# Four linear layers on one core: two products of layer 0 and the up projection change places in TensorE's order

## The reference, cut to what matters

```
x = x + (x @ W0[subject].T + b0[subject])            # layer 0, 512 x 512
x = x + rotate_pairs_of_rows(x, amplitudes ** dt, frequencies * dt)   # layer 1
x = x + (x @ W2[category] + b2[category])            # layer 2, 512 x 512
h = relu(x @ W1[language] + b1[language])            # layer 3, 512 -> 128
y = x + (h @ Wup[language] + bup[language])          #          128 -> 512
x = x + layernorm(y) * gamma[language] + beta[language]
```

## Time and profile before

| | |
|---|---|
| median of 3 runs | 1144.45 us (1143.76 to 1145.31) |
| the profiled execution | 1143.54 us, of which the span from first to last instruction is 1141.1 us |
| TensorE matmuls busy | 1102.6 us, 97% of the span |
| VectorE busy | 916.4 us, 80% |
| ScalarE busy | 778.7 us, 68% |
| GpSimd busy | 677.9 us, 59% |
| mean granted clock of TensorE | 0.992 |
| DMA | 353.5 MB, 310 GB/s on average |

### The profile page before, as it was taken

How to read it: one execution, slowest core, us unless ns; L and a number is a source line. 1 busy time by engine, 2 the same in 40 slices (tenths; PEclk the granted TensorE clock), 3 DMA queues, 4 the chain that set the end, 5 groups by cost and what they waited for, 6 DMA issues and landing times.

```text
span 1141.1 us, 28378 instructions
## 1 busy us (share of the span) xinstructions
PE 1102.6 (97%) x6046; PEld 924.0 (81%) x6046; DVE 916.4 (80%) x1373; ACT 778.7 (68%) x1824; POOL 677.9 (59%) x807
## 2 busy tenths in 40 slices
PE   4799999999999999999999999999999999999996
PEld 2588888888788888888888888887888888787885
DVE  7787787778987787778978877878877878888876
ACT  3476776767676776767767666767767767676764
POOL 5756556557755656556656556566556566565563
PEclk9899999999999999999999999999999999999999
DMA  7898979897998999799989889988998999798882
GB/s 247 307 330 302 321 284 334 315 309 277 381 338 295 322 316 315 269 351 327 333 303 361 307 275 341 323 300 308 356 310 286 342 316 356 263 369 323 312 297 70
DMA packets 97554, 353.50 MB, mean 310 GB/s; under 512 B 11870, under 2 KB 12510, under 8 KB 79932
## 3 DMA queue, kind: packets, MB, share of 16 engines
q1 hardware_dynamic: 95756, 350.39, 86.7%
q10 hardware_dynamic: 1584, 0.93, 0.3%
HBM read 316.94 MB, written 34.34 MB: 308 GB/s over the span
## 4 chain that ended last, share of the span: by engine, by line
PE 92%; DVE 2%; issue 2%; ACT 1%; DMA 1%; POOL 1%; DVEq 0%; SPq 0%; POOLq 0%; ACTq 0%
PE ps_mix L1075 10%; PE ps_l L1064 10%; PE ps_l L1100 10%; PE ps_l L1048 10%; PE ps_l L1094 10%; PE ps_l L1090 10%; PE ps_hT L1120 9%; PE ps_l L1059 5%; PE ps_x3T L1110 5%; PE ps_l L1052 5%; PE ps_y L1133 3%; PE ps_y L1131 3%; PE ps_y L1130 3%; DVE w_lo L873 1%; DMA x_in<-xT 1%
## 5 line engine op out<-in xcount | busy, mean ns | idle before, releaser
L595 ACT ACTIVATE w_hi<-w_in 128x1024 fp32r<-128x1024 f32 x256 | 270.8, 1058 | 219.5 <-POOL w_in L469 219.5
L873 DVE TENSOR_TENSOR w_lo<-w_in,w_hi 128x1024 fp32r<-128x1024 f32 x256 | 333.7, 1303 | 19.8 <-ACT w_hi L595 18.1
L482 POOL TENSOR_SCALAR var_eps<-square_sum 128x1 f32<-128x1 f32 x128 | 24.4, 191 | 414.5 <-DVE w_lo L873 307.9
L902 DVE TENSOR_TENSOR x<-ps_l,rows 128x512 f32<-128x512 f32 x126 | 87.0, 691 | 124.3 <-PE ps_l L1100 124.3
L640 ACT ACTIVATE x3T<-ps_x3T,minus_bup 128x128 f32<-128x128 f32 x512 | 145.8, 366 | 49.3 <-PE ps_x3T L1110 48.0
L508 POOL TENSOR_TENSOR x_beta<-x,rows 128x512 f32<-128x512 f32 x128 | 168.8, 1319 | 0.0
L476 POOL TENSOR_TENSOR x_lo<-x_in,x_hi 128x512 fp32r<-128x512 f32 x127 | 164.1, 1292 | 7.5 <-ACT x_hi L571 7.5
L469 POOL TENSOR_TENSOR w_in<-w_in,ident 128x512 f32<-128x512 f32 x128 | 166.5, 1301 | 2.9 <-DMA w_in<-W 2.9
L1075 PEld LDWEIGHTS ps_mix<-mix,x 128*128 128x128 f32 x1024 | 125.0, 192 | 32.9 <-issue 32.8
L1048 PE MATMUL ps_l<-w_hi,x_hi 128*128 128x512 f32 x512 | 150.2, 415 | 0.0
L1075 PE MATMUL ps_mix<-mix,x 128*128 128x128 f32 x1024 | 141.9, 282 | 4.9 <-DVE x L883 4.9
(11 more groups left out here) (148 smaller groups left out, 1843.7 us busy)
## 6 DMA issues: line engine op xcount, KB each, us to landing
w_in<-W SPq DMA_DIRECT2D x128, 1024.0 KB, 6.6
rows<-sample_rows SPq DMA_DIRECT2D x128, 768.0 KB, 7.1
x_in<-xT SPq DMA_DIRECT2D x128, 256.0 KB, 6.2
w_in<-W SPq DMA_DIRECT2D x128, 256.0 KB, 5.0
out<-yb SPq DMA_DIRECT2D x128, 256.0 KB, 6.6
w_in<-W0T SPq DMA_DIRECT2D x7, 1024.0 KB, 5.5
wup_sb<-Wup SPq DMA_DIRECT2D x1, 2560.0 KB, 13.7
w_in<-W0T SPq DMA_DIRECT2D x4, 512.0 KB, 6.4
```

The costliest lines, as they stand in the source:

```text
L595: act.activation(w2_hi[:, halves[n]], w2_in[s % WB][:, halves[n]], ACT.Copy).then_inc(w2_hi_made, 1)
L873: dve.tensor_tensor(w2_lo[:, half], w2_in[s % WB][:, half], w2_hi[:, half].bitcast(fp32), ALU.subtract).then_inc(w2_lo_made, 1)
```

## The change

`l0_back` loses its first two matmuls, which become `l0_middle`. `l2` is cut in two behind L1094: `l2_front` and `l2_back`. In the loop TensorE now takes `l0_middle(s + 1)` between the two. The load of the language offset moves with it, ahead of `l0_middle`. From s = 2 on the up projection comes ahead of the transposes; at s = 1 their order stays. What each stage computes and waits for is the same, and so are the instructions of all other engines.

```diff
-            def l0_back(s):
-
+            def l0_middle(s):
 
                 for c in range(C // 2, C):
                     pe.matmul(ps_l0[:, :], x_lo[s % 2][:, c * N:(c + 1) * N], w0_hi[s % 2][:, c * D:(c + 1) * D],
                               start=False, stop=False)
+
+            def l0_back(s):
+
+
                 for c in range(C):
...
-            def l2(s):
+            def l2_front(s):
...
                 mm.then_inc(l2_hi_done, 1)
+
+            def l2_back(s):
+
                 for c in range(C):
...
             for s in range(1, B):
                 if s < LAST:
                     l0_front(s + 1)
-                l2(s)
+                l2_front(s)
+                here = language_offset(pe, s - 1)
+                if s < LAST:
+                    l0_middle(s + 1)
+                l2_back(s)
                 if s == 1:
                     sort_coefficients()
-                here = language_offset(pe, s - 1)
                 if s < LAST:
                     l0_back(s + 1)
-                transpose_x3(s)
                 if s == 1:
+                    transpose_x3(s)
                     pe.wait_ge(wup_hi_made, len(wup_parts))
                     pe.wait_ge(wup_lo_made, len(wup_parts))
                     pe.wait_ge(coef_made, 2)
                 up(s - 1, here)
+                if s > 1:
+                    transpose_x3(s)
                 if s < LAST:
                     rotate(s + 1)
                 down(s)
```

More of the change, by code:

```diff
@@ L1135, in _ @@
             l0_front(0)
+            l0_middle(0)
             l0_back(0)
@@ L1139, in _ @@
             gather_rows()
-            l2(0)
+            l2_front(0)
+            l2_back(0)
             gather_beta()
@@ L1143, in _ @@
             l0_front(1)
+            l0_middle(1)
             l0_back(1)
```

## The result

| | before | after |
|---|---|---|
| median | 1144.88 us (4 runs) | 1179.37 us (4 runs, 1179.09 to 1180.61) |
| ratio | | 1.0303, 95% interval 1.029 to 1.0315 |
| profiled execution, its span | 1143.54, 1141.1 us | 1179.35, 1177.4 us |
| median time from rotation to rotation | 8.43 us | 8.73 us |

What follows compares the result with a forecast made beforehand. TensorE's fixed matmul chain bounds the kernel, with no cover for x1 at the rotation. 117 x 0.30 = 35.1 plus 0.8 us for slow steps gives 35.9; on 1143.54 that is 1179.4, stated as 1180, range 1172 to 1200.

Steps and rivals of the forecast that it cites:

- What bounds it: Steady step: a fixed chain of TensorE matmuls, 8.44 us between rotations, with no cover left for x1 at the rotation.
- A slack of about 0.16 us: DVE's chain L902, L935, L883 to x1 could come about 0.16 us later before the change.
- x1 did cost: Rotation's weight load before the change: its wait for x1 was said to cost almost nothing, with gaps in 123 steps.
- L883 overlaps L935 by 0.08: DVE's queue after the change: L883 starts 0.08 before L935 ends, as L935 does with L902.
- E: The end of layer 2 in a step, from which the prediction counts its times in us.
- the rival of 1189 us: DVE's queue: L883 doesn't overlap L935, so the step grows by 0.37 or 0.38 us; 1189 us, chance 0.14.
- Rotation at E + 2.18, a step of 0.29: Rotation's first matmul waits for x1 until E + 2.18 against 1.89 us of work; step grows 0.29, taken as 0.30.
- The slow steps: The 8 steps not steady: h_lo's wait makes them lose 0.1 rather than gain 0.36, together 0.8 us.
- The transposes cost nothing as long as x1 holds the rotation back: Transposes just ahead of the rotation: copies of x3T keep 0.2 us of slack before the down projection's fourth chunk.
- The floor beneath: Down projection: if x1 were early, the x3T copies bind, 0.1 a step, 12 us, 1156 us; rival's chance 0.04.
- What would show it: New profile: TensorE idle before rotation released by x1, 0.3 us a step, 30 to 40 us together; 8.74 between rotations.
- The clock: TensorE: its clock falls because it idles in every step; 80 us, 1260 us, chance 0.02.

Runs made afterwards that it cites:

- x1 first: VectorE makes x1 (finish_l0) ahead of finish_norm: 1146.34 us in the kernel before the change, 1157.53 us in the kernel after it.
- the late wait written first: The kernel before, with the wait for l0_done written first in finish_l0: 1140.9 us, ratio 0.9968.
- the last experiment: The kernel after, with GpSimd making h_lo ahead of the fold of the next W2: 1178.19 us, ratio 1.0296.
- part 1 alone: The kernel after, with the transposes back ahead of the up projection, so only the two x_lo products are moved: 1178.29 us, ratio 1.0298.
- part 2 alone: The kernel before, with only the up projection put ahead of the transposes: 1153.41 us, ratio 1.0086.
- part 1 with x1 first: The kernel before, with the two x_lo products moved and VectorE making x1 ahead of finish_norm; transposes stay ahead of up: 1157.97 us, ratio 1.012.

## Why the prediction was right, point by point

- **What bounds it.** A fixed chain of matmuls with no cover left at the rotation: right. Counted from rotation to rotation, 116 steps grew by 0.30 each, 34.9 of the span's 36.3 us.
- **"A slack of about 0.16 us".** Right as far as tested: one small operation used up 0.08 of it without any cost to the step, and a move of one product, 0.23, cost 0.07. x1 first gained the steady step nothing in the kernel before. "Costs almost nothing" was a little low: x1 did cost 0.03 a step, as the late wait written first showed.
- **L883 overlaps L935 by 0.08.** Forecast E + 1.31 for its start and E + 2.00 for its end; measured E + 1.31 and E + 1.99. This refutes the rival of 1189 us. The Trainium skill, "VectorE: DVE Perf Modes", section "The DRAIN you can't avoid", has the next operation start when the pipe is empty; the rows of this step have two pairs that start 0.08 ahead of the listed end. Its section "Two Vector instructions with no wait between them" allows such a start to an instruction that isn't held, and with that the trace agrees. By the first rule alone, at the price that the rival gives, the kernel would have taken 1189 us.
- **Rotation at E + 2.18, a step of 0.29.** Two errors that cancelled. The load came 0.11 behind x1 and the matmul 0.03 behind the load, not 0.12 and 0.06: E + 2.13, which is 0.24 by itself. The other 0.06 lie behind the rotation: from it to the end of the next layer 2 it took 6.10 us before and 610.87 - 604.26 - 0.45 = 6.16 after. Half of that is in the rotation: with its first load later, its first matmul to that of down is 0.97 (604.26 to 605.23 in that timeline) instead of 0.94. Most of the rest is in the x2T_hi products, 0.93 instead of 0.91 from their first to the first x2T_lo product; why is open. I hadn't priced either.
- **The slow steps.** "0.1 each, 0.8 us together": wrong, and the sum came out by luck. The seven steps with a new W0 changed by -0.5 to +0.2 us and are 0.4 us shorter together. What the span has beyond the steady steps is the one step at the start, 2.0 us longer at the lower granted clock, where the prediction had "changes of a tenth". The mechanism (w_lo's wait shrinks, h_lo's appears) is in the rows; as the last experiment shows, it is worth about 1 us.
- **"The transposes cost nothing as long as x1 holds the rotation back".** Right in this kernel (part 1 alone and both parts differ by 1 us). The floor beneath is real, too: part 2 alone stands on it, and so does x1 first. Its price was somewhat high, 0.1 a step and 12 us for 0.07 and 8 us: the copies' signal is there 0.06 behind their end, not 0.1. That x1 first came out near the 1156 us of that rival (1157.5) is partly luck, since some 5 us of it lie in the slow steps and at the start.
- **"What would show it".** Wrong in one place: I had said that TensorE's idle time would be listed as released by x1. The waits list it as a gap of the *weight load*, "issue", 34.1 us against 26.9, only 7 us more; 2.2 of 230 us show up as idle of PE. The sure signs were the time from rotation to rotation, and the number of matmuls in a stretch. DVE's wait before L902 grew to 1.61, its steady wait for the up projection is gone, and w_lo's waits fell from 5.7 to 1.7 us, all as said.
- **The clock** stayed at 1.00 in the even stretch though TensorE loses 0.3 us in each step. What it did cost is the 2 us at the start, behind an idle time of 4.5 us that both kernels have. The Trainium skill, "TensorE: Matmul & The Clock Gate", section "A second HAM failure mode: psum-queue depth-cycling", describes a kernel in which short idles between groups let the clock swing; the ones here didn't.

What failed clearly were two expectations behind the prediction, for part 2 alone and for part 1 with x1 first. Both took away the wait that bound and assumed nothing close behind it. With one part or the other in place, three chains are late by little: x1 by 0.24 us (part 1), x3 into the transposes by 0.13 (part 1 without part 2), the copies of x3T by 0.06 (part 2).

## What to carry to other kernels

When two products change places on the engine that bounds the kernel, its own work stays the same and its consumers' deadlines don't: count, from the end of each product that someone waits for, how much work is left before the result comes back, and compare it with the whole queue of the consumer (here 1.89 us against 2.13). Do it for every chain that closes within a few tenths, since a fix for one only uncovers the next. And look at how many instructions a stretch holds, not at how busy it reads: part 1 alone is 230.00 of 230 us busy and 3% slower.

## What the runs showed of the hardware

- **The order in which waits are written costs time.** In `finish_l0` the wait written first is the one that the trace shows on the instruction; the later one is a semaphore instruction of its own ahead of it. With the late event on the separate one, DVE started 0.11 us behind it; with it on the instruction itself, 0.04. On ACT's copies the same swap gave about 0.05 (0.74 instead of 0.79 behind the first transpose). In the kernel before, this is 0.3% (1144.4 to 1140.9 us).
- **A short operation costs its start-to-start distance.** A copy of 128 x 16 is listed at 0.17 us and delays the next by 0.08.
- **DVE's w_lo beside POOL's x_beta.** Both read SBUF. Overlapping by 0.13 us (604.64 against 604.77, above) w_lo takes 1.22; started together it takes 2.34 (578.45, above), 1.12 more for 1.25 of overlap; in the earlier trace rows 0.98 of overlap gave 2.07, 0.85 more. So past the first 0.13 DVE takes longer by as much as the two overlap. The Trainium skill, "SBUF — State Buffer", section "SBUF: two separate sides", calls the shared port an exclusive lock for the whole instruction; apart from the first 0.13 these numbers agree.
